# The last group's hats along the rows formed on ScalarE in SBUF, in a four-layer convolution kernel

## The reference, cut to what matters

```python
off = conv3x3(out, off_w, off_b).reshape(B, 9, 2, H, W); dy, dx = off[:, :, 0], off[:, :, 1]
py = hh + ky + dy                     # (B, 9, 14, 14), a real row for each tap and place
px = ww + kx + dx
val = v00*wy0*wx0 + v01*wy0*wx1 + v10*wy1*wx0 + v11*wy1*wx1   # bilinear sample, 0 outside the grid
out = einsum("bckhw,ock->bohw", val, w) + b
```

## Time and profile before

| | |
|---|---|
| median of 3 runs | 1062.71 us (1061.28 to 1067.7) |
| profiled execution, its own time | 1064.98 us |
| its span, first to last instruction | 1062.8 us |
| TensorE busy | 922.9 us (87%) |
| VectorE busy | 734.4 us (69%) |
| ScalarE busy | 550.9 us (52%) |
| GpSimd busy | 355.4 us (33%) |

### The profile page before, as it was taken

The page is one execution under the profiler, slowest core; times in us unless marked ns, Lnnn a source line. Parts: engine busy times, 40 slices in busy tenths (PEclk is TensorE's granted clock), DMA queues, the critical chain, the costliest instruction groups (busy, mean ns, idle before and its releaser), DMA issues.

```text
span 1062.8 us, 19419 instructions
## 1 busy us (share of the span) xinstructions
PE 922.9 (87%) x7272; PEld 630.8 (59%) x7272; DVE 734.4 (69%) x2047; ACT 550.9 (52%) x1155; POOL 355.4 (33%) x320
## 2 busy tenths in 40 slices
PE   4687889999999999999999999999999998875843
PEld 2455556666766676666666666766676665544422
DVE  2566458687878787878788786878787868555332
ACT  1142453655657474747484755657474746361512
POOL 2012332425151615243342425151615242333100
PEclk9685979999999999999999998999999999896866
DMA  9101153252625353535444361625353534335060
GB/s 222 31 12 40 35 135 122 76 179 65 180 83 169 96 167 95 162 109 139 132 118 155 93 184 56 179 83 169 95 173 92 142 118 130 121 96 160 13 198 15
DMA packets 116545, 123.30 MB, mean 116 GB/s; under 512 B 64802, under 2 KB 99750, under 8 KB 116454
## 3 DMA queue, kind: packets, MB, share of 16 engines
q1 hardware_dynamic: 107812, 105.46, 34.2%
q0 software_dynamic: 6144, 13.71, 4.6%
q10 hardware_dynamic: 2498, 2.91, 1.2%
HBM read 84.32 MB, written 37.73 MB: 115 GB/s over the span
## 4 chain that ended last, share of the span: by engine, by line
PE 36%; DVE 28%; ACT 17%; issue 9%; POOL 4%; DMA 4%; SPq 1%; ACTq 1%; POOLq 0%; DVEq 0%
PE ps L620 33%; DVE c_w L1283 6%; ACT L968 3%; ACT d_pad L968 3%; ACT y L968 3%; DVE x L1291 2%; DVE b_xf L1291 2%; ACT x L968 2%; POOL b_res L1197 2%; DVE st L1318 2%; DVE y L1288 2%; DVE b_md L1283 2%; ACT c_hat L968 1%; SPq L1806 1%; DVE y L1291 1%
## 5 line engine op out<-in xcount | busy, mean ns | idle before, releaser
L1245 POOL DMA_INDIRECT b_yp<-y_turned,b_to x64 | 87.1, 1361 | 289.1 <-DMA y_turned<-b_yt 274.4
L620 PE MATMUL ps<-y,inw 128*128 128x392 f32 x384 | 138.2, 504 | 0.0
L1318 DVE BATCH_NORM_STATS2 st<-x 128x6 f32<-128x196 f32 x256 | 73.7, 352 | 88.9 <-POOL x L1197 76.6
L1197 POOL TENSOR_TENSOR rs<-ve,root 128x4 f32<-128x4 f32 x64 | 65.8, 1028 | 203.4 <-DVE ve L1287 202.9
L620 PE MATMUL ps<-c_w,c_zt 126*64 126x196 f32 x896 | 90.9, 352 | 23.6 <-DMA c_zt<-z_turned 10.6
L1283 DVE TENSOR_TENSOR c_w<-c_w,c_hat 126x1176 f32<-126x1176 f32 (+1 forms) x64 | 97.8, 1582 | 13.0 <-DMA c_w<-hat_turned 13.0
L620 PEld LDWEIGHTS ps<-y,inw 128*128 128x128 f32 x384 | 70.3, 193 | 42.3 <-issue 2.5
L620 PEld LDWEIGHTS ps<-c_w,c_zt 126*64 126x64 f32 x896 | 65.2, 145 | 44.5 <-issue 29.3
L620 PE MATMUL ps<-w,a_S 128*32 128x384 f32 (+2 forms) x1280 | 84.2, 403 | 6.3 <-DVE a_S L1291 6.3
L968 ACT ACT_TABLE_LOAD x50 | 64.2, 1283 | 38.3 <-PE ps L620 37.5
L1219 POOL DMA_INDIRECT x_turned<-b_xt,b_to x64 | 63.3, 989 | 34.7 <-DVE b_xt L1294 20.0
(11 more groups left out here) (203 smaller groups left out, 2092.2 us busy)
## 6 DMA issues: line engine op xcount, KB each, us to landing
c_w<-hat_turned SPq DMA_DIRECT2D x32, 771.8 KB
c_w<-hat_turned SPq DMA_DIRECT2D x32, 578.8 KB
z_turned<-c_z SPq DMA_DIRECT2D x32, 441.0 KB
c_zt<-z_turned SPq DMA_DIRECT2D x16, 882.0 KB
b_xp<-x_turned SPq DMA_DIRECT2D x32, 222.0 KB
x<-in_x SPq DMA_DIRECT2D x32, 196.0 KB, 2.7
y_turned<-b_yt SPq DMA_DIRECT2D x32, 196.0 KB
out<-x SPq DMA_DIRECT2D x32, 196.0 KB
```

The source lines that it names most:

```text
L620: return nc.tensor.matmul(o, l, r, start=start, stop=stop)
L1197: return nc.gpsimd.tensor_tensor(out=o, in0=x, in1=y, op=op)
L1245: nc.gpsimd.indirect_dma_start(out=YP[:, m, h].rearrange("p b d -> p (b d)"), out_offset=None, in_=y_dram[g % 2], in_offset=bass.IndirectO ...
L1318: last = nc.vector.bn_stats(st[s][:, 2 * c + b, :], x[:, c, b, :])
```

## The change

For group 15 alone, the store to `hat_turned` and the four loads from it are left out, and ScalarE makes the px hats of `c_w` itself. A third block of the constant `expand` expands px without subtracting the grid index, so each of the 126 rows holds px of its tap (`wide[half(b), 2 * x if final(g) else x, :]`). ScalarE copies that to `c_hat[b][:, 1]`, and the Abs and Relu for the py half cover 196 columns instead of 392. Then, in a new step `f2`, i = 6 with four parts, it writes |px - v| for each column v of the part (6 or 8 Abs of 126 x 196, the bias a number in the instruction) and one Relu of 1 - that over the whole part. The other 15 groups are as before, but `expand` has 126 columns more for everyone.

```diff
@@ shape_constants
-    expand = np.zeros((128, 2, TAPS, HW), f)
+    expand = np.zeros((128, 3, TAPS, HW), f)
...
             expand[at + 2, 1, k] = k % 3 - 1 - np.arange(HW)
+            expand[at + 2, 2, k] = k % 3 - 1
@@ PARTS, PLAN: "scalar", "f2"
-    ... 5: 4},
+    ... 5: 4, 6: 4},
-    ... 284562, 288735),
+    ... 284562, 288735, 296524, 296824,
+        310161, 310261),
@@
+def final(g):
+
+    return g == GROUPS - 1
@@ tensor, f2
-                            last = mm(tiles[b][0:TV, x * N:(x + 1) * N], wide[half(b), x, :], c_off[half(b), :])
+                            last = mm(tiles[b][0:TV, x * N:(x + 1) * N], wide[half(b), 2 * x if final(g) else x, :], c_off[half(b), :])
@@ scalar, f2
+                    t = R.tile(("ex", b), g)
+                    if final(g):
+                        fn(c_hat[b][:, 0, :], t[0:TV, 0:N], ACT.Abs)
+                        fn(c_hat[b][:, 1, :], t[0:TV, N:2 * N], ACT.Copy).then_inc(R.drained(("ex", b), g), 1)
+                    else:
...
                 if i == 4:
                     drained(act, ("ex", b), g)
-                    x = c_hat[b][:, :, :]
+                    x = c_hat[b][:, 0, :] if final(g) else c_hat[b][:, :, :]
                     fn(x, x, ACT.Relu, scale=-1.0, bias=1.0).then_inc(c_hat_ok.sem, 1)
...
+                if i == 6 and final(g):
+                    h, b = part // G, part % G
+                    if part == 0:
+                        filled(act, "acc", g - 1, H)
+                    drained(act, ("ex", b), g)
+                    cols = VSPLIT[h]
+                    for vx in range(cols.start, cols.stop):
+                        ins = fn(c_w[b][:, vx, :], c_hat[b][:, 1, :], ACT.Abs, bias=-float(vx))
+                    ins.then_inc(c_apart[part], 1)
+                    act.wait_ge(c_apart[part], 1)
+                    x = c_w[b][:, cols, :]
+                    fn(x, x, ACT.Relu, scale=-1.0, bias=1.0).then_inc(c_near[part], 1)
@@ vector, d2
-                    v.wait_ge(*hat_in[b][h].at(g))
+                    if final(g):
+                        v.wait_ge(c_hat_ok.sem, c_hat_ok.count(g, b + 1))
+                        v.wait_ge(c_near[part], 1)
+                    else:
+                        v.wait_ge(*hat_in[b][h].at(g))
@@ sync, f2 and d2
-                if i == 5:
+                if i == 5 and not final(g):
...
-                if i == 0:
+                if i == 0 and not final(g):
                     load_hats(sp, part, 0, g)
-                if i == 2:
+                if i == 2 and not final(g):
                     load_hats(sp, part, 1, g)
                 if i == 1:
+                    if final(g):
+                        filled(sp, "acc", g - 1, H)
```

More of the change, by code:

```diff
@@ L95, in shape_constants @@
             for k in range(TAPS):
-                expand[at + 2 * k, 0, k] = expand[at + 2 * k + 1, 1, k] = 1
+                expand[at + 2 * k, 0, k] = expand[at + 2 * k + 1, 1:, k] = 1
         at = b * MID + 2 * TAPS
         ground[at], ground[at + 1], ground[at + 2] = t // HW, t % HW, 1
-        expand[at, 0] = expand[at + 1, 1] = 1
+        expand[at, 0] = expand[at + 1, 1:] = 1
         for k in range(TAPS):
@@ L278 @@
         (),
-        (256260, 256978, 258101, 260941, 261413, 261413, 261413, 263153, 265143, 284562, 288735),
+        (256260, 256978, 258101, 260941, 261413, 261413, 261413, 263153, 265143, 284562, 288735, 296524, 296824,
+        310161, 310261),
         (316724, 316724, 316724),
@@ L583, in build @@
         hat_out = [landed(f"hat_out{b}") for b in range(G)]
+        c_apart = [sem(f"distances{k}") for k in range(2 * G)]
+        c_near = [sem(f"hats_along_row{k}") for k in range(2 * G)]
         hat_in = [[landed(f"hat_in{b}_{h}") for h in range(2)] for b in range(G)]
@@ L877, in f2 @@
                     tiles = [take(("ex", b), g) for b in range(G)]
-                    wide = k128("expand").rearrange("p (x k) -> p x k", x=2)
+                    wide = k128("expand").rearrange("p (x k) -> p x k", x=3)
                     for x in range(2):
                         for b in range(G):
-                            last = mm(tiles[b][0:TV, x * N:(x + 1) * N], wide[half(b), x, :], c_off[half(b), :])
+                            last = mm(tiles[b][0:TV, x * N:(x + 1) * N], wide[half(b), 2 * x if final(g) else x, :], c_off[half(b), :])
                             if x == 1:
@@ L1106, in f2 @@
                     filled(act, ("ex", b), g)
-                    fn(c_hat[b][:, :, :].rearrange("p x n -> p (x n)"), R.tile(("ex", b), g)[0:TV, 0:2 * N], ACT.Abs)\
-                        .then_inc(R.drained(("ex", b), g), 1)
+                    t = R.tile(("ex", b), g)
[3 more added lines that the diff above has]
+                    else:
+                        fn(c_hat[b][:, :, :].rearrange("p x n -> p (x n)"), t[0:TV, 0:2 * N], ACT.Abs)\
+                            .then_inc(R.drained(("ex", b), g), 1)
                 if i == 4:
                     drained(act, ("ex", b), g)
-                    x = c_hat[b][:, :, :]
+                    x = c_hat[b][:, 0, :] if final(g) else c_hat[b][:, :, :]
                     fn(x, x, ACT.Relu, scale=-1.0, bias=1.0).then_inc(c_hat_ok.sem, 1)
```

## The result

The changed kernel takes 1052.98 us (median of 17 runs, 1041.56 to 1060.48), the kernel before 1061.6 beside it (17 runs, 1054.85 to 1072.56). The ratio over the runs without a disturbance is 0.9897, interval [0.9872, 0.9922]. The profiled execution took 1054.14, its span is 1052.3. By the ratio the gain is 1.03%, by the two medians 0.8%; the prediction had given 0.03 to a gain of more than 1%.

What follows compares the result with a forecast made beforehand. The last load of hats was taken to bound the last group, through the last product and second sum. An earlier second sum (-6.2) and larger constant load (+0.2) gave -6.0 on 1062.71: 1056.7 us, range 1053.0 to 1061.0.

Steps and rivals of the forecast that it cites:

- I carry the difference to the median: Whole kernel: apply the traced execution's 6.0 us gain to the median of three earlier runs, 1062.71, giving 1056.7.
- ScalarE's parts: ScalarE, last group: 2.87 us per h = 0 part, 3.71 per h = 1 part, the last ending at 1025.4.
- VectorE's cover: VectorE, last group: group 14's operations and three products finish 1.2 us before the fourth starts; group 14's delay costs nothing.
- `c_zt`: Load ahead of TensorE's first sum: has 8.0 us from its issue, taken as landed in time.
- The second sum: TensorE, last group: starts at 1027.3, ends at 1031.4 as the middle of two cases, 6.2 us earlier than before.
- the two cases: TensorE's second sum: clock rises after 28 matmuls, ending 1030.4, or the pause starts the count afresh, ending 1032.3.
- a rise at the very start: TensorE's second sum: if the clock rises as it begins, the kernel's time is 1056.
- 25.2 us of tail ... that the change does not touch: Behind the second sum to the span's end at 1062.8: stays 25 us as before.
- this fall at the 1 x 1 convolution: Rival, tail: clock stays down through the second sum and falls before this convolution, up to 0.9 us more; chance 0.07.
- The start: Load of constants: `expand` grows by 126 columns, 64.5 kB, adding 0 to 0.26 us, taken as 0.2.
- ScalarE becomes the bound: Rival, last group: at 0.52 us per Abs the kernel is slower, 1065.0; it loses from 0.445; chance 0.04.
- `c_zt` did not take the hats' place: Rival, first sum: `c_zt` lands no earlier than now, gain 4.1 to 6.3 us, 1056.6 to 1058.8; chance 0.08.

Runs made afterwards that it cites:

- e5: The change timed and profiled a second time, against the kernel before: ratio 0.9939 [0.9905, 0.9972], median 1052.93 us over 12 runs.
- e2: The change with the third `expand` block placed behind all other constants, against the kernel before: ratio 0.9918 [0.9887, 0.9949], 6 runs.
- e8: The change with all four ScalarE parts moved ahead of group 14's `d_h` and `d_o`: last group's first `c_hat` to end 58.3 us.
- e3: The change without ScalarE's four parts, px hats left out in the last group: first `c_hat` to end 47.1 us, the change 51.1.
- e7: The change plus padding matmuls, with VectorE forming and multiplying part h = 0 of sample 0: ratio 0.9905 [0.9866, 0.9945] against the kernel before.
- e11: e7 with ScalarE's first own part (h0 b1) moved ahead of group 14's `d_h`: ratio 0.9912 [0.9873, 0.9952] against the kernel before.
- e1: The kernel before with only the third block added to the constant `expand`: ratio 0.9984 [0.9956, 1.0012], median 1061.23 us over 12 runs.
- e4: The change with each of the 28 Abs done twice: last group's first `c_hat` to end 59.9 us, 2.7 more than the kernel before.

## Why the prediction missed, point by point

**The direction and the mechanism held; the sum's base and its range did not.** The failed step is "I carry the difference to the median: 1062.71 - 6.0 = 1056.7", with the lower end of 1053.0. That end was set by three runs of the kernel before, 1.4 under to 5.0 over their median; 17 lie from 6.8 under to 11.0 over theirs. That the time falls 0.02 us outside and not inside is chance: the two runs next to the median took 1052.16 and 1053.75. The miss of 3.7 us against the forecast divides so:
- 1.1 is the base: 17 runs gave 1061.6 where three had given 1062.71 (in the later comparisons 1057.98 to 1062.57).
- 0.6 is the sum: to the end of the span the three profiles with loads take 57.2, 55.8 and 59.0 us (mean 57.3), the three of the change 51.1, 50.4 and 50.7 (mean 50.75). That is 6.6 where 6.2 less 0.2 was forecast; against the one profile that the sum was worked from it is 6.1.
- 0.4 lies outside the span, which the sum left unchanged. In the 29 timed runs of the change (the first comparison and e5) the execution takes 1.77 to 1.98 us longer than its span, in every run of a kernel with loads that has a span on record at least 2.13. Why is open.
- 1.6 is left for the scatter of whole executions, which the range allowed for too little. In the profiles the same first fifteen groups end between 994.4 and 1011.1.

6.6 us is 0.62%, a ratio of 0.9938, and 7.0 with the 0.4 outside the span is 0.9934. Both are inside the intervals of the repeat and of e2 and outside the first comparison's. All comparisons taken together, 113 runs with loads and 27 of the change, the means differ by 8.0 us (± 1.6), though the chips are not equally represented. The recorded clocks fit it: over 98 runs with loads, of before and of the constant alone, the span falls by 8.0 us for each 0.01 of mean granted clock, and the change's 27 runs lie 4.0 (± 1.1) us under that line. Taking 6.6 us at 0.50 out of a mean of 0.9345 raises the mean by 0.0027, another 2.2 by the line: 6.2 in all, as an estimate. So what the first comparison had beyond is ascribed, not shown, to executions with more or less half clock in the earlier groups. Which of them fell there can't be told, since one execution of a run is traced.

**ScalarE's parts: right.** Six Abs 1.65 and 1.63 (forecast 5 x 0.256 + 0.367 = 1.65), eight 2.15, the Relus 1.18 and 1.51 (1.19 and 1.51); end at 19.62 where 19.8 was forecast. The price of 0.27 lies between the bounds of 0.22 and 0.52.

**VectorE's cover: right.** Its operations of group 14 ended at 14.17 (14.2), and it had 1.28 us to spare (1.2). e8 shows what the loss of that cover costs.

**`c_zt`: right.** In the change nothing waits for it; where something does, the sum starts 5.7 us behind its issue (e3), 5.4 in e7 and 5.3 in e11 (8.0 allowed).

**The second sum: right in kind, mis-sized.** The pause of 0.5 us did not start the rise afresh, which was the one of the two cases with the lower bound of 3.1 us: the clock rose 1.2 us, some 8 matmuls, into the second sum, where that bound had four. 3.45, 3.01 and 3.42 us were measured where the middle, 4.1, was taken. The count of 28 matmuls did not carry over: in e2, with the same lists, the clock rose 0.3 us, some 2 matmuls, into this sum, and in e1, with loads and the long pause, some 18 into it. For a rise at the very start the prediction's own terms give 1055.4 (32 x 0.0885 = 2.8 us, 7.5 earlier less 0.2), not the 1056 that it names.

**"25.2 us of tail ... that the change does not touch": wrong by 0.5 to 0.9.** It took 26.1, 25.8 and 25.7. The clock, up some 8 us earlier against `c_hat`, was at half again earlier and did not rise behind the 3 x 3 convolution, so 8 matmuls took 1.68 for 0.93. The text had looked for this fall at the 1 x 1 convolution, which kept its 0.93. This and the shorter second sum nearly cancel, so that the sum comes as near as it does is partly luck.

**The start: 0.2 forecast, nothing measured** (-0.16% and +0.3%, either interval with no change in it). Intervals of some 3 us to either side cannot tell 0.2 us, so this term stays open.

**The rivals.** That ScalarE becomes the bound is true in so far as its last part is what the last product waits for (e4), but at 0.27 us per Abs, not at the 0.445 from which the change would lose. In e7 VectorE formed a part: a single add of 126 x 196 is cheaper there, 0.185 in a row against 0.27 for ScalarE's Abs, but the absolute value, 1 - that, and the cut at zero with the product took three more passes. The part took 4.64 busy us with the product in it, against 2.83 on ScalarE and 1.38 for the product. The Trainium skill, page "ScalarE: Activation LUTs", section "Rules for kernel authors", has relu and add belong on VectorE, with a figure for bf16. The single add agrees with it, the whole part in fp32 does not; no run here is in bf16. Moving a part to VectorE gains 1.2 us here, in time in which VectorE was idle. `c_zt` did not take the hats' place.

## What to carry to other kernels

At the end of a kernel, where no other group covers a wait, a round trip through DRAM can be swapped for work on an engine that stands idle there: price the work by the nearest rows, then look in the strict lists for what stands behind it and what ahead, since there e8 lost the whole gain. When executions of one program scatter by 15 us, measure a change of 6 us in the stretch that it touches, over several profiles, and make the range of the total as wide as the scatter. Time won by an earlier clock rise may be paid back behind it, as 0.75 us was here, so follow the clock to the end of the span.

## What the runs showed that was not expected

- Loads land unevenly, activations don't: the last product waited for its load until 25.16, 25.11 and 26.99 us after `c_hat`, for ScalarE until 19.72, 19.71 and 19.73.
- Padding in the tail's pauses held the full clock there: the 3 x 3 convolution took 2.21 us instead of 4.19, the tail 22.5 instead of 26.1. A pause of 2.35 or 2.67 us ahead of the second sum was followed by half clock in most of it (4.55), although in e11 the first sum had just run at full clock (2.21); after e7's pause of 0.60 the sum kept full clock (2.87).
- The same 3 x 3 convolution of 4.19 us was followed by full clock in the kernel before and by half clock in the change, three times of three, but by full clock again in e4, a version of the change whose second sum ended later. In the kernel before the rise came just as the convolution ended at 1054.19: the window from 1054 to 1055 has a mean clock of 0.94. What decides it stays open.
